# Attention times values computed transposed, with 1/sum moved into the sum with x, in a two-stage attention and expert kernel

## The reference

```python
q, k_new, v_new = x @ wq.T, x @ wk.T, x @ wv.T      # x after layer norm
k = concatenate([ctx, k_new]); v = concatenate([ctx, v_new])
attn = softmax(q @ k.T / sqrt(512))
x = x + (attn @ v) @ wo.T
x = x + experts(layernorm(x))
```

## Time and profile before

| | before |
|---|---|
| median of 3 runs | 474.01 us (472.74 to 474.7) |
| profiled execution | 473.97 us |
| its span | 472.2 us |
| PE busy | 445.1 us (94%) |
| PE weight loads busy | 402.1 us (85%) |
| DVE busy | 298.2 us (63%) |
| ACT busy | 208.4 us (44%) |
| POOL busy | 98.5 us (21%) |
| mean granted TensorE clock | 0.979 |

### The profile page before, as it was taken

One profiled execution on the slowest core, in us unless ns is written; L12 is line 12 of the kernel. 1 busy time (PEld: TensorE's weight loads), 2 busy tenths in 40 slices (PEclk: granted clock), 3 DMA queues, 4 the chain that ended last, 5 costly groups with the idle time before them and its releaser, 6 DMA issues.

```text
span 472.2 us, 7695 instructions
## 1 busy us (share of the span) xinstructions
PE 445.1 (94%) x2991; PEld 402.1 (85%) x2991; DVE 298.2 (63%) x525; ACT 208.4 (44%) x281; POOL 98.5 (21%) x122
## 2 busy tenths in 40 slices
PE   2989999999999878999999999999999999999991
PEld 2967888887888668999999999999999999999990
DVE  5665737636643655777677766766766776776630
ACT  3457524434623523435444444444345345445401
POOL 5006062543425624000200201101102002002002
PEclk9999999999999986999999999999999999999997
DMA  8974995514545172955955955955955855856203
GB/s 239 399 204 134 250 229 171 157 40 130 187 125 208 59 266 94 326 169 197 272 165 191 276 171 181 280 181 174 267 198 165 265 194 186 256 183 197 52 1 49
DMA packets 26911, 88.41 MB, mean 187 GB/s; under 512 B 2560, under 2 KB 8704, under 8 KB 26880
## 3 DMA queue, kind: packets, MB, share of 16 engines
q1 hardware_dynamic: 23296, 80.13, 52.0%
q0 software_dynamic: 3584, 7.88, 8.1%
HBM read 73.55 MB, written 14.45 MB: 186 GB/s over the span
## 4 chain that ended last, share of the span: by engine, by line
PE 86%; DVE 4%; POOL 3%; ACT 3%; issue 2%; DMA 1%; POOLq 0%; ACTq 0%
PE PJ L222 15%; PE PJ L224 15%; PE PJ L223 15%; PE SC L222 4%; PE SC L224 4%; PE SC L223 4%; PE SC L396 3%; PE SC L397 3%; PE SC L398 3%; PE T L396 3%; PE T L397 3%; PE T L398 3%; POOL vl L1059 2%; PE T L230 2%; PE R L230 1%
## 5 line engine op out<-in xcount | busy, mean ns | idle before, releaser
L224 PE MATMUL PJ<-eh,ul 128*128 128x256 f32 x504 | 142.2, 282 | 0.0
L223 PE MATMUL PJ<-el,uh 128*128 128x256 f32 x504 | 142.1, 282 | 0.0
L222 PE MATMUL PJ<-eh,uh 128*128 128x256 f32 x504 | 142.1, 282 | 0.0
L720 DVE TENSOR_TENSOR ul<-ng,uh 128x1536 fp32r<-128x1536 f32 x64 | 112.5, 1758 | 11.4 <-ACT uh L513 11.4
L223 PEld LDWEIGHTS PJ<-el,uh 128*128 128x128 f32 x504 | 96.3, 191 | 2.6
L222 PEld LDWEIGHTS PJ<-eh,uh 128*128 128x128 f32 x504 | 95.9, 190 | 2.7
L224 PEld LDWEIGHTS PJ<-eh,ul 128*128 128x128 f32 x504 | 96.0, 190 | 0.0
L513 ACT ACTIVATE uh<-ng 128x1536 fp32r<-128x1536 f32 x64 | 94.8, 1483 | 0.0
L668 ACT ACTIVATE hs<-PJ 128x256 f32<-128x256 f32 x64 | 24.6, 384 | 152.2 <-PE PJ L224 148.9
L971 DVE TENSOR_TENSOR hf<-PJ,hs 128x256 f32<-128x256 f32 x64 | 27.2, 424 | 70.6 <-ACT hs L668 70.6
L1121 POOL DMA_INDIRECT out<-ys,yidx x16 | 27.3, 1707 | 199.8 <-ACT ys L663 197.4
(11 more groups left out here) (185 smaller groups left out, 756.6 us busy)
## 6 DMA issues: line engine op xcount, KB each, us to landing
ng<-in_units SPq DMA_DIRECT2D x64, 768.0 KB, 4.4
vs<-in_ctxn SPq DMA_DIRECT2D x8, 768.0 KB, 4.7
kTs<-in_ctxT SPq DMA_DIRECT2D x8, 750.0 KB, 4.8
slots<-zero SPq DMA_DIRECT2D x8, 514.0 KB, 11.9
xe<-slots SPq DMA_DIRECT2D x8, 514.0 KB, 4.5
wTs<-in_weights SPq DMA_DIRECT2D x8, 512.0 KB, 9.9
out<-x_all SPq DMA_DIRECT2D x8, 224.0 KB, 4.4
x_all<-in_x SPq DMA_DIRECT2D x1, 896.0 KB, 15.6
```

The source lines that it names most:

```text
L222: nc.tensor.matmul(o, lh(k), rh(k), start=k == 0, stop=False)
L223: nc.tensor.matmul(o, lh(k), rl(k), start=False, stop=False)
L224: last = nc.tensor.matmul(o, ll(k), rh(k), start=False, stop=k == n - 1)
L720: v.tensor_tensor(o, whole, hi.bitcast(F32), ALU.subtract).then_inc(s, 1)
```

## The change

`pe_attn` takes the values as the stationary operand, in four blocks of 128 feature columns, and the transposed exponentials as the moving one, 112 columns. The result comes out with features on partitions, as `pe_wo` wants it. `on`, `do_o` and `pe_oT` go; `hi_o` and `lo_o` read the product's bank. The division by the sum moves behind the product with wo, into the sum with x, as one `scalar_tensor_tensor`. The three waits for `v_lo`, one ahead of each context tile, become one ahead of the whole product. The place of `on` in memory stays reserved.

```diff
@@ -264,21 +264,19 @@
             pe.wait_ge(a_lo, g + 1)
             pe.wait_ge(vn_lo, g + 1)
-            o = bank[0:S, :]
-            nc.tensor.matmul(o, aTh[a][0:S, 0, :], vnh[a][:, :], start=True, stop=False)
-            nc.tensor.matmul(o, aTh[a][0:S, 0, :], vnl[a][:, :], start=False, stop=False)
-            nc.tensor.matmul(o, aTl[a][0:S, 0, :], vnh[a][:, :], start=False, stop=False)
-            for j, n in enumerate(CROWS):
-                pe.wait_ge(v_lo, 3 * g + j + 1)
-                nc.tensor.matmul(o, aTh[a][0:n, j + 1, :], vh[a][0:n, j, :], start=False, stop=False)
-                nc.tensor.matmul(o, aTh[a][0:n, j + 1, :], vl[a][0:n, j, :], start=False, stop=False)
-                last = nc.tensor.matmul(o, aTl[a][0:n, j + 1, :], vh[a][0:n, j, :], start=False, stop=j == 2)
+
+            vp = [(S, vnh[a], vnl[a], 0)] + [(n, vh[a], vl[a], r) for r, n in enumerate(CROWS)]
+            pe.wait_ge(v_lo, 3 * (g + 1))
+            for m in range(KT):
+                c = slice(128 * m, 128 * m + 128)
+                for j, (n, h, l, r) in enumerate(vp):
+                    o = bank[:, S * m:S * m + S]
+                    wh = h[0:n, c] if j == 0 else h[0:n, r, c]
+                    wl = l[0:n, c] if j == 0 else l[0:n, r, c]
+                    nc.tensor.matmul(o, wh, aTh[a][0:n, j, :], start=j == 0, stop=False)
+                    nc.tensor.matmul(o, wh, aTl[a][0:n, j, :], start=False, stop=False)
+                    last = nc.tensor.matmul(o, wl, aTh[a][0:n, j, :], start=False, stop=j == CT)
             last.then_inc(attn, 1)
-
-        def pe_oT(pe, g, a, bank):
-            pe.wait_ge(attn_out, g + 1)
-            transposes(bank, [(S * k, on[a][:, 128 * k:128 * k + 128], S, 128)
-                              for k in range(KT)]).then_inc(o_T, 1)
...
-                pe_oT(pe, A, 0, T[1])
...
-                pe_oT(pe, B, 1, T[2])
...
-            def do_o(g, a, bank):
+            def hi_o(g, a, bank):
                 act.wait_ge(attn, g + 1)
-                act.wait_ge(sum_inv, g + 1)
-                nc.scalar.activation(on[a][:, :], bank[0:S, :], ACT.Copy, scale=rinv[:, a, :]).then_inc(attn_out, 1)
-
-            def hi_o(g, a, bank):
-                act.wait_ge(o_T, g + 1)
...
-                do_o(A, 0, PJ[0])
+                hi_o(A, 0, PJ[0])
...
-                do_o(B, 1, PJ[1])
-                hi_o(A, 0, T[1])
+                hi_o(B, 1, PJ[1])
...
-                hi_o(B, 1, T[2])
...
                 dve.wait_ge(wo_mm, g + 1)
-                v.tensor_tensor(x_all[:, g, :], bank[0:S, :], x_all[:, g, :], ALU.add).then_inc(x2_ok, 1)
+                dve.wait_ge(sum_inv, g + 1)
+                v.scalar_tensor_tensor(x_all[:, g, :], bank[0:S, :], rinv[:, a, :], x_all[:, g, :],
+                                       ALU.mult, ALU.add).then_inc(x2_ok, 1)
...
-                lo_o(A, 0, T[1])
+                lo_o(A, 0, PJ[0])
...
-                lo_o(B, 1, T[2])
+                lo_o(B, 1, PJ[1])
```

More of the change, by code:

```diff
@@ L145, in build_kernel @@
         ex = [sb(f"ex{a}", [S, 512], F32) for a in range(2)]
-        on = [sb(f"on{a}", [S, D], F32) for a in range(2)]
+        top[0] += 2 * D * 4
         x2T = [at(f"x2T{a}", [128, KT, S], F32, top[0] + a * KT * S * 4) for a in range(2)]
@@ L203, in build_kernel @@
         a_T, a_hi, a_lo = sem("a_T"), sem("a_hi"), sem("a_lo")
-        attn, attn_out = sem("attn"), sem("attn_out")
-        o_T, o_hi, o_lo = sem("o_T"), sem("o_hi"), sem("o_lo")
+        attn = sem("attn")
+        o_hi, o_lo = sem("o_hi"), sem("o_lo")
         wo_mm, x2_ok = sem("wo_mm"), sem("x2_ok")
```

## The result

The changed kernel takes 503.65 us (503.57 to 505.73), the kernel before beside it 474.36 us: a ratio of 1.063 (95% interval 1.060 to 1.067), 29.3 us more. The forecast was 492.7 us with a range up to 498.5. So the direction was right, and 11 us more than forecast have to be explained. The profiled execution took 503.62 us, its span 501.9.

A forecast was written before the change was run, and what follows sets the result against it. TensorE was taken as the bound in attention pairs 1 and 2, with pairs 0 and 3 summed separately. 6.38 + 8.64 + 3.71 = +18.7 us on 473.97 gave 492.7 us, range 489.2 to 498.5.

The forecast's parts named there:

- the clock: TensorE's clock: no new fall priced into the forecast, only some 2 us either way at 172 us.
- the sum: Attention stage: pair 0 +6.38, pairs 1 and 2 +8.64, pair 3 +3.71, total +18.7 us.
- Rival 5: Pair 0: clock falls once, behind 2.6 us of new idle time; up to +4.9 us, 497.6 us; 6%.
- Rival 4: All eight products: thin matmuls let the clock fall, up to 39 us more, 532 us; with half, 512; 5%.
- The price of the product: Each batch's product: 48 matmuls at 111.3 ns, set by weight loads; 5.34 us against 2.79, +2.55.
- Rival 1: Product: moving columns set the distance, loads hidden; 66 ns a matmul, 475.5 us; 4%.
- rival 2: Product: loads hidden in part beside a short moving operand; 82 ns a matmul, 481.5 us; 4%.
- Rival 3: Product: load left out where the stationary operand repeats; 32 loads, 3.56 us a batch, 478.5 us; 4%.
- The transposes: Each batch: four transposes of `on` go, saving 0.39 us of TensorE.
- The moved wait: Pair 0: first product starts at 40.51 instead of 37.84, waiting for all of `vl`; free in other pairs.
- The scale: x2_stats with one more operand: equal duration, 0.68 us; on the path only in pair 3, at most +0.6.
- Pair 3's chain: Pair 3's end: VectorE late through `lo_u`, not TensorE; x2_stats B 2.97 us behind A, +3.71 us.

The follow-up runs named there:

- b_wait: Kernel before, with only the moved wait: all three parts of `vl` awaited ahead of the product; 476.25 us, ratio 1.004.
- b_keep_early: Kernel before, with unused 512-column matmuls in TensorE's idle times at pair 3's end and ScalarE's early copy of the first values; 470.67 us, ratio 0.991.
- a_early: Changed kernel, with ScalarE's copy of the first batch's values moved ahead of the first exponential, removing the gap in pair 0; 496.88 us, ratio 1.046.
- b_keep: Kernel before, with unused 512-column matmuls filling TensorE's idle times at the end of pair 3; 471.58 us, ratio 0.991.
- a_fill: Changed kernel, with five unused 512-column matmuls in the 1.1 us idle time ahead of pair 3's last product; 498.94 us, ratio 1.051.
- a_early_fill: Changed kernel, with ScalarE's early copy of the first values and five unused 512-column matmuls ahead of pair 3's last product; 494.62 us, ratio 1.037.
- a_ef_again: The same kernel as a_early_fill, run again with more executions; 489.61 us, ratio 1.033.
- a_twice: a_early_fill, with the product of B in pair 1 issued twice in a row (96 thin matmuls, no gap); 493.63 us, ratio 1.043.
- a_keep: Changed kernel, with ScalarE's early copy and unused 512-column matmuls (5, 2, 9 and 3) in the idle times at pair 3's end; 487.05 us, ratio 1.024.

## Why the prediction was wrong

**The step that failed is the clock, a term that the sum has at nothing.** The sum takes 111.3 ns, the distance at full clock, for all 384 thin matmuls; 10.7 of the 11 us that were missed are two stretches in which they stand 213 ns apart. Rival 5 had the right place and mechanism for pair 0: a gap of 2.6 us ahead of a thin product, the clock falls once, up to 4.9 us more. It measured 5.0, and that the two agree so well is luck: rival 5 had the whole product at half clock, but the clock fell 1.9 us into it, so that 3.1 us were lost in the product and the rest in the transposes and the projection behind it. And I gave it 6%, and named one place only. The second, in pair 3, stood in my own sum: there I let the product of B begin 1.84 us behind the transposes "as before", with its 1.08 us of idle time, and put 5.41 us of thin matmuls behind it without asking the same question. It cost 5.7 us. Rival 4 put the thin product alone at fault, in all eight; in the changed kernel's profile the six products without a gap ahead of them kept the full clock, and the experiments without gaps show one such fall in a trace. What a gap alone does (b_wait, b_keep_early) is a fall of 3.4 us; why the thin product then holds the clock down isn't shown by any run. The range took in one fall, up to 498.5, and two happened: 492.7 + 5.0 + 5.7 = 503.4.

**The price of the product: right.** 111.3 ns a matmul and 5.34 us, measured 5.31 in the block that follows no transposes (pair 0 B) and 5.38 else. The distance doesn't depend on whether 112 or 224 columns stream. Rival 1 (66 ns) and rival 2 (82 ns) are out; the figure of some 81 ns in the Trainium skill ("TensorE: Matmul & The Clock Gate", "Back-to-back issue gap") doesn't hold for these fp32r operands, and its rule for a load (section "LDWEIGHTS (loading the stationary operand)"), columns / 1.2, is again 4.6 ns short. Rival 3 (a load left out for a repeated operand) is out too: all 48 stand equally far apart, 3247 loads for 3247 matmuls.

**The transposes: right.** From the product of B in pair 1 to the product of B in pair 3 the time grew by 22.60 - 13.92 = 8.68 us. Four products at +2.55 less four blocks of transposes at 0.39 are 8.64.

**The moved wait: right in size, 2.50 us, wrong in what it sets off.** I had priced it as lost time only (+2.1 us). a_early shows what it costs with the fall: 6.8 us (8.4 by the ratios).

**The scale: right**, 0.06 us for each sum, within the bounds, and no time.

**Pair 3's chain.** I said that `lo_u` would be late, not TensorE. At half clock TensorE was late: x2_stats A waits 1.04 us for the matmuls with wo, until 193.50. The distance to x2_stats B is 3.04 us, 2.97 were forecast.

## What to carry to other kernels

Turning a product so that its result comes out transposed saves the transposes, but count the weight loads: at 128 fp32r stationary columns a matmul took 111 ns here at full clock, with 112 and with 224 moving columns alike, so 48 matmuls with 112 moving columns take nearly twice as long (5.34 us) as 12 with 512 (2.79 us). And cost a thin product at both levels of the clock wherever an idle gap stands ahead of it, for each such place, also where the gap is an old one. Unused thick matmuls in the gaps are a cheap cure, and are worth trying in a kernel that has no thin products at all. They are no sure one: in one of seven executions of b_keep_early the clock fell behind a gap that the profiles of the kernel before and of b_keep don't have, and again behind the fillings.

## What the hardware showed unexpectedly

- An idle gap of 1.1 us ahead of a product with 47 of 111 ns of streaming was followed by a stretch of 13.6 us at half clock; the same gap ahead of matmuls with 512 columns (the kernel before) was followed by none.
- Gaps of 2.50 us (b_wait, 512 columns behind it) and 1.95 us (b_keep_early, transposes and 224 columns) were followed by 3.4 us at half clock each. Where a fall came in or ahead of a thin product, the stretch lasted 10.2 or 13.6 us, and in all five of them in the profiles (two in the changed kernel, one each in a_early, a_fill and a_early_fill) the clock came back only 3.1 to 6.0 us behind the product's end, never in it.
- At half clock the load of 128 columns takes twice as long as well: the thin matmuls stand 213 ns apart (41 steps from 179.56 to 188.30 in 8.74 us).
- Without a gap, 10.75 us of thin matmuls kept the full clock, and yet in one execution of another kernel it fell after 3.2 us of them. What decides that stays open; nothing here names it. Of 20 executions of the thin kernels without gaps (a_early_fill, a_ef_again, a_twice, a_keep) three were long, two by some 6 us and one by 13, and only one of the three has a trace.
